# A decoder layer on one core: second norm in the drain of cross attention, a reordered first stage, and other banks for the side jobs of attention

## The reference

```
x = layernorm(x + ssm(x))              # xp = x W_in^T, dt = softplus(W_dt xp + b), a = exp(-dt exp(logA)), scan, W_out
x = layernorm(x + cross_attn(x, ctx))  # 16 heads, 8 kv heads, 1024 keys of width 256
h = x + self_attn(rmsnorm(x, w1))      # 16 heads, 4 kv heads, causal, rotary
x = layernorm(h + moe(rmsnorm(h, w2))) # 8 experts, 2 per row
```

## Time and profile before

| | us |
|---|---|
| three runs | 1571.29, 1569.46, 1571.0; median 1571.0 |
| profiled execution: its own time | 1574.32 |
| its span, first to last instruction | 1571.8 |
| mean granted TensorE clock | 0.942 |

### The profile page before, as it was taken

How to read it: one execution, slowest core, us unless ns; L and a number is a source line. 1 busy time by engine, 2 the same in 40 slices (tenths; PEclk the granted TensorE clock), 3 DMA queues, 4 the chain that set the end, 5 groups by cost and what they waited for, 6 DMA issues and landing times. The chain is left out here.

```text
span 1571.8 us, 25227 instructions
## 1 busy us (share of the span) xinstructions
PE 1387.9 (88%) x8067; PEld 740.1 (47%) x8067; DVE 1051.2 (67%) x1984; ACT 814.1 (52%) x1462; POOL 385.7 (25%) x585
## 2 busy tenths in 40 slices
PE   7888999999999999972879999997569999999971
PEld 4344444444444444431445555553336666666640
DVE  5747777777777777746577868785485655555654
ACT  5447666666666666633265656555244453444420
POOL 5302020201111110104464646542460000000024
PEclk9899999999999999985989999998779999999986
DMA  8217767575767676747234435344426454455334
GB/s 246 38 47 135 141 107 153 108 152 111 149 114 146 114 146 114 134 88 293 49 70 79 116 65 128 62 92 83 168 94 236 167 190 148 185 197 184 101 91 127
DMA packets 422079, 203.17 MB, mean 129 GB/s; under 512 B 369361, under 2 KB 383697, under 8 KB 422001
## 3 DMA queue, kind: packets, MB, share of 16 engines
q1 hardware_dynamic: 418224, 191.75, 50.4%
q0 software_dynamic: 3200, 10.49, 2.2%
q10 hardware_dynamic: 576, 0.00, 0.0%
HBM read 90.33 MB, written 18.55 MB: 69 GB/s over the span
## 5 line engine op out<-in xcount | busy, mean ns | idle before, releaser
L1188 DVE SCALAR_TENSOR_TENSOR xa_PN<-xa_SC,xa_rs,xa_PN 128x1024 f16<-128x1024 f32 x128 | 164.4, 1284 | 98.4 <-issue 97.7
L1076 ACT ACTIVATE xa_PN<-xa_SC,xa_rs 128x1024 f16<-128x1024 f32 x128 | 147.1, 1149 | 113.4 <-POOL xa_rs L916 113.4
L980 PE MATMUL xa_psS<-xa_KT,xa_QT 128*128 128x512 f16 x768 | 186.4, 379 | 6.4 <-DVE xa_mn L1201 5.0
L992 PE MATMUL xa_psO<-xa_PT,xa_V 128*128 128x512 f16 x768 | 173.5, 383 | 10.3 <-DMA xa_PT<-xa_PN 10.3
L916 POOL TENSOR_SCALAR xa_rs<-xa_rc,flag 128x1 f32<-128x1 f32 x128 | 34.2, 267 | 523.5 <-DVE xa_rc L1181 523.5
L1201 DVE CUSTOM_DVE_ANT_0 xa_SC<-xa_psS,maskb 128x1024 f32<-128x1024 f32 x128 | 155.2, 1212 | 4.5 <-PE xa_psS L980 2.4
L1098 ACT ACTIVATE xa_SC<-xa_SC,xa_mn 128x1024 f32<-128x1024 f32 x128 | 145.4, 1136 | 13.9 <-DVE xa_mn L1201 13.8
L1557 PE MATMUL rmoe_psG<-rmoe_XGT,W 128*128 128x352 f16 x768 | 126.8, 315 | 8.4 <-DVE rmoe_HF L1662 6.8
L1557 PE MATMUL rmoe_psU<-rmoe_XGT,W 128*128 128x352 f16 x768 | 125.6, 313 | 2.4 <-issue 2.4
L1572 PE MATMUL rmoe_psY<-W,rmoe_HT 128*128 128x512 f16 (+1 forms) x576 | 126.8, 379 | 0.0
L1662 DVE TENSOR_TENSOR rmoe_HF<-rmoe_psU,rmoe_SG 128x352 f32<-128x352 f32 x64 | 33.6, 525 | 137.5 <-ACT rmoe_SG L1614 133.3
(11 more groups left out here) (232 smaller groups left out, 2419.9 us busy)
## 6 DMA issues: line engine op xcount, KB each, us to landing
W13raw<-in_L_ffn_w_dram SPq DMA_DIRECT2D x16, 2048.0 KB, 12.1
W2raw<-in_L_ffn_w_dram SPq DMA_DIRECT2D x8, 2048.0 KB, 8.3
expert_rows_dram<-zeros SPq DMA_DIRECT2D x11, 512.0 KB, 8.7
xa_WPraw<-in_L_xattn_Wq_dram SPq DMA_DIRECT2D x8, 512.0 KB, 4.9
xa_WOraw<-in_L_xattn_Wo_dram SPq DMA_DIRECT2D x8, 512.0 KB, 4.5
sa_WPraw<-in_L_ffn_wq_dram SPq DMA_DIRECT2D x4, 1024.0 KB, 6.7
sa_WOraw<-in_L_ffn_wo_dram SPq DMA_DIRECT2D x4, 1024.0 KB
expert_out_dram<-rows SPq DMA_DIRECT2D x16, 256.0 KB, 2.2
```

The source lines that it names most:

```text
L980: last = nc.tensor.matmul(psS[j % NSC][:, c:c + cw], QT[b][:, hq, g, t * P:(t + 1) * P], KT[b][:, hk, c:c + cw], start=(q == 0), stop=(q = ...
L992: last = nc.tensor.matmul(psO[:, c:], V[b][:, hv, blk, :], PT[g % NPT][:, blk, hp, c:], start=(blk + q == 0), stop=(blk == NBLK - 1 and q ...
L1076: nc.scalar.activation(PN[j % NPN][:, 0:w // P, 0, :], by_block(SC[j % NSC], w), ACT.Identity, scale=rs[:, j % 4:j % 4 + 1]).then_inc(norm ...
L1188: nc.vector.scalar_tensor_tensor(out=PN[j % NPN][:, 0:w // P, 1, :], in0=by_block(SC[j % NSC], w), scalar=rs[:, j % 4:j % 4 + 1], in1=PN[j ...
```

## The change

Three things. (1) The first stage is reordered. DVE does the mask's work before the step that needs `WZ`; ACT casts all four pieces of `wout` early; POOL splits `xa_WP` before the context, and starts the last three of its four context pieces only when both `step_low` are done (a wait on `dt_lo`); eight buffers for `dec` (laid over `win` and `winN`) free batch 1's decays from batch 0's scans, and PE spreads batch 1's steps earlier. (2) The phase "n2" is gone. Its work is a tail of cross attention: batch 0's tiles are normed by DVE and POOL while the last `PN` tiles are turned; PE transposes them between `values` and the last output tiles; batch 1's tiles are normed as their output tiles are added. The square sum on ACT is replaced by arithmetic on the variance (one short POOL instruction more per tile, none on ACT). `sa_WP` is loaded in the last kv head's first half and split by ACT and POOL in the last half, steps 2 to 7. The copies of the normed tiles now precede the 14 DMAs of zeros in SP's list. `PN` and `CN` lie over `X2`, the copies' target. (3) The bank table of the side jobs differs between the batches, for both attentions, and in self attention three of the four `wo` jobs stand one step later.

```
-            for n in range(DC, 2 * DC):                                          # ACT
-                decay(n)
+                decay(DC + n)
...
+            for b in range(B):                                                   # POOL, after xa_WP
+                pool.wait_ge(c_in[b], 16)
+                for q in range(2):
+                    if b or q:
+                        pool.wait_ge(dt_lo, B)
...
-    BANK = (0, 1, 2, 0, 1, 2, 0, 1, 2, 1)
-    BACK = (3, 2, 3, 3, 3, 3, 3, 3, 3, 2)
+    BANK = ((0, 1, 2, 0, 1, 2, 0, 2, 1, 0), (2, 1, 0, 2, 1, 0, 2, 0, 1, 2))
...
-                 5: ([("proj", 4)], []), 6: ([("proj", 5)], []), 8: ([("wo", 0)], []), 10: ([("wo", 1)], []),
-                 12: ([("wo", 2)], []), 14: ([("wo", 3)], [])}
+                 5: ([("proj", 4)], []), 6: ([("proj", 5)], []), 9: ([("wo", 0)], []), 11: ([("wo", 1)], []),
+                 13: ([("wo", 2)], []), 14: ([("wo", 3)], [])}
...
+    def jobs_back(h, k, last):
+
+        if isinstance(h, int) and h == 1 and k < 2:
+            return k + 1
+        return 3 if last else (3, 3, 3, 3, 3, 3, 3, 2, 4, 3)[k]
...
+            if tail is not None:                                                 # SP
+                for t in range(TPB):
+                    sp.wait_ge(landed[t], 16 * 2 * kv_heads * groups)
+                for i in range(NT):
+                    sp.wait_ge(ln_done, i + 1)
+                    sp.dma_start(keep[:, i, :], X[:, i, :]).then_inc(kept, 16)
+                for dst, src, arrived in clear:
+                    sp.dma_start(dst, src).then_inc(arrived, 16)
+                sp.wait_ge(kept, 16 * NT)
...
+            if tail is not None:                                                 # PE
+                for i in range(TPB):
+                    norm_pe(pe, i)
             for t in range(TPB):
                 h = 2 * kv_heads - 1
-                output(h, 1, t, jobs_before(h) + JO + t, ring[(t + 1) % NJ])
+                output(h, 1, t, jobs_before(h) + JO + t, psJ[(1, 0, 2, 1)[t]])
+            if tail is not None:
+                for i in range(TPB, NT):
+                    norm_pe(pe, i)
...
             for t in range(TPB):                                                 # DVE
                 h = 2 * kv_heads - 1
-                output_add(h, 1, t, jobs_before(h) + JO + t, ring[(t + 1) % NJ])
+                output_add(h, 1, t, jobs_before(h) + JO + t, psJ[(1, 0, 2, 1)[t]])
+                if tail is not None:
+                    norm_stats(TPB + t)
+                    if 0 < t < TPB - 1:
+                        norm_apply(TPB + t - 1)
+            if tail is not None:
+                norm_dve(dve, TPB)
+                norm_apply(NT - 2)
+                norm_apply(NT - 1)
...
-            phase_norm(nc, "n2", X, identF, XT=XT, norm_w=norm1_w, keep=X2, fetch=loads + cleared)
...
+                          tail=(norm1_w, X2, own_weights, own_loads, cleared))
```

More of the change, by code:

```diff
@@ L427, in _ @@
                 tr_act(act, n)
-            for m in range(2, DC):
-                nc.scalar.copy(woutN[:, m, 0, :], wout[:, m, :]).then_inc(woutN_hi, 1)
             act.wait_ge(small_in, 32)
@@ L1125, in half @@
                         piece_high(*piece[:2])
+                    if last and tail is not None and 0 <= j - NWO < len(next_pieces):
+                        dst, src = next_pieces[j - NWO]
+                        if j == NWO:
+                            act.wait_ge(next_in, 16 * len(next_loads))
+                        nc.scalar.copy(dst[:, 0], src).then_inc(next_hi, 1)
             if not ready:
@@ L1142, in _ @@
                 pass
+            if tail is not None:
+                for i in range(NT):
+                    norm_act(act, i)
         @block.vector
@@ L1221, in half @@
                     jobs(h, b, j, first, last, 1)
+                    if last and tail is not None and j == NS:
+                        for i in range(TPB):
+                            norm_stats(i)
+                        for i in range(TPB):
+                            norm_apply(i)
             for i, (dst, src) in enumerate(wp_pieces if not ready else []):
@@ L1881, in decoder_layer @@
             cleared.append((YG[at:at + w, :], zeros[0:w, :], zeroed))
-        with ExitStack() as cross:
-            CT = cross.enter_context(nc.sbuf_tensor("CT", [P, 2, DCTX // P, B * S2], F16))
-            maskb = cross.enter_context(nc.sbuf_tensor("maskb", [P, B, S2], F32))
-            weights, loads = attention_weights(nc, cross, "xa", 2, DCTX // P, xWq, xWk, xWv)
-            phase_ssm(nc, X, XT, CT, x, ctxt, mask, W_in, W_out, log_A, W_dt, b_dt,
-                      (identF, causal, maskb, flag, ropeC, ropeS, zeros), rope_in, weights, loads)
-            attention(nc, "xa", X, XT, CT, identF, weights, xWq, xWk, xWv, xWo, 8, 2, S2,
-                      lambda b, t: maskb[:, b, :], flag, None, ready=True)
@@ L1891, in decoder_layer @@
[L1891 to L1898 removed]
+        X2 = sb("X2", [P, NT, D], F32)[:]
@@ new lines, in decoder_layer @@
+        with ExitStack() as own:
+            own_weights, own_loads = attention_weights(nc, own, "sa", 4, DC, wq, wk, wv)
+            with ExitStack() as cross:
+                CT = cross.enter_context(nc.sbuf_tensor("CT", [P, 2, DCTX // P, B * S2], F16))
+                maskb = cross.enter_context(nc.sbuf_tensor("maskb", [P, B, S2], F32))
+                weights, loads = attention_weights(nc, cross, "xa", 2, DCTX // P, xWq, xWk, xWv)
+                phase_ssm(nc, X, XT, CT, x, ctxt, mask, W_in, W_out, log_A, W_dt, b_dt,
+                          (identF, causal, maskb, flag, ropeC, ropeS, zeros), rope_in, weights, loads, X2)
+                attention(nc, "xa", X, XT, CT, identF, weights, xWq, xWk, xWv, xWo, 8, 2, S2,
+                          lambda b, t: maskb[:, b, :], flag, None, ready=True,
+                          tail=(norm1_w, X2, own_weights, own_loads, cleared))
+            attention(nc, "sa", X, XT, XT, identF, own_weights, wq, wk, wv, wo, 4, 4, S,
+                      lambda b, t: causal[:, S - (t + 1) * P:S], None, (ropeC, ropeS), ready=True)
```

163 lines of the change are left out of this document (115 added, 48 removed).

## The result

The changed kernel takes 1544.9 us (1544.7 to 1546.8, four runs) beside 1570.2 (1566.9 to 1571.3) on the same chip: a ratio of 0.984, 95% interval [0.9825, 0.9857], so 25.3 us less. The forecast was 1548, with a range of 1537 to 1558. The profiled execution took 1544.87, its span 1542.7 against 1571.8, the mean granted clock 0.951 against 0.942.

The account below looks back on a forecast made before the run. PE is about nine tenths busy, so only its waits or half-clock stretches count. First stage -7, boundary -15, weights' split +1, banks +1 and self attention -3 sum to -23: 1548 us against 1571.0, range 1537 to 1558.

Parts of the forecast that it names:

- First stage: Start of the kernel: earlier scans, decays and outputs from the reordering save 7 us, bounds -11 and -4.
- `scan_low`: First stage, before batch 1's scans: four DVE instructions beside POOL's context pieces take 7.5 us, between 3.3 and 8.
- mask work ahead of `WZ`: First stage: three DVE instructions moved to where DVE waited for `WZ` cost 0, or 1 if cover is short.
- Boundary: Cross attention's end to self attention's first projection: norm in the drain saves 15 us, bounds -25 and -11.5.
- the list: SP's 14 DMAs of zeros at the boundary, behind the last copy at 714.7: 13.3 us, SP through at 728.
- Weights' split and banks: Cross attention: splitting `sa_WP` beside the last half costs 1 us (0 to 3), the new banks 1 (0 to 4).
- Rival D: Cross attention: the job at k = 7 waits for a late V split; at 2 us a half +4, 1575; chance 0.05.
- Self attention: Later `wo` 0 fills part of each wait, -2, and a spared slow clock gives -1: -3, bounds +1 and -10.
- The clock's part: Self attention: a shorter wait may spare one group of slow matmuls after it, -1.
- rival C: Self attention keeps its clock in every half: another -7 there, 1541; chance 0.10.
- Rival A: SP's queue takes the zeros faster when empty, so the boundary gives -25: 1538; chance 0.14.
- Rival B: First stage gives nearly nothing, as POOL's context pieces run beside `scan_low` and outputs start late: -1, 1554; chance 0.15.

Follow-up runs that it names:

- a1: The changed kernel again, unaltered, on the chip where the first stage's single edits ran; 1545.5 us beside 1571.3 for the kernel before.
- m1: The changed kernel with the mask's instructions back in their old places in the first stage; 1547.4 us beside 1571.3 for the kernel before.
- h1: The changed kernel with the same bytes of zeros in 9 DMAs instead of 14; 1527.3 us beside 1558.9 for the kernel before.
- h2: The changed kernel with every second of the 14 DMAs of zeros issued by ACT, the others by SP; 1526.3 us beside 1558.9 for the kernel before.
- b1: The changed kernel with one bank table for both batches and the old distances, slots staying new; 1532.8 us beside 1558.9 for the kernel before.
- s1: The changed kernel with self attention's four `wo` jobs back at steps 8, 10, 12, 14; 1536.0 us beside 1557.2 for the kernel before.
- x1: The changed kernel without the mask's move, POOL's wait on `dt_lo`, and batch 1's early spread and decays; 1539.6 us beside 1558.9 for the kernel before.
- z1: The changed kernel with its 14 DMAs of zeros moved behind transposes in self attention's second half; 1520.8 us beside 1557.2 for the kernel before.
- o1: The changed kernel with two loops swapped, so SP issues the zeros before the eight copies; 1520.5 us beside 1557.2 for the kernel before.

## Why the prediction was right, and where it was off

The direction and its three sources hold, with the boundary as the largest; the time is 3.1 us below the forecast. By its own steps:

- **First stage, -7: -8.9.** By other pairs of profiles it is -6 to -11, as slow matmuls fall on one or the other. Scans at 39.1, as computed from the decays; batch 1's and the outputs within 1.5 us. The term that was mis-sized is `scan_low`, 7.5 us for four: they took 5.3. The price beside a neighbour was right or even low (1.44 and 2.60 us, where I had 1.9); the number was wrong. I had put a context instruction beside each of the four, but POOL did four of its six beside the decays and the scans, which they hardly slow (4.65 us for four scans; 4.55 for the next four, with POOL idle). By the Trainium skill (SBUF — State Buffer, section "SBUF: two separate sides") the port that DVE and GpSimd share is an exclusive lock, and I had worked out 9 us for four and -5 for the stage from it. The trace agrees with it as a mechanism: the first two `scan_low` end 0.54 us behind the context cast and the context subtraction that they met (45.09 against 44.55, 47.62 against 47.08). My sum by it failed by the same count. The mask work ahead of `WZ` was costed at 0 and delayed it by about 1 us (21.7 in a1, 20.9 in m1), inside its bound.
- **Boundary, -15: -11.7.** Compute was done 27.5 us behind `values` (27 to 27.8 forecast), the last copy was issued 23.7 behind it (23.5). The step that failed is the list: "five go at once (3.5 us) and nine at 1.1 to 1.28: 13.3 us". Four went in 3.6 us and ten at 1.3: 16.6, the 16.7 that the earlier trace rows had measured. I had made the queue emptier than before by what stood ahead of the zeros, and had taken the lowest rate of the range for the rest; but from the fourth DMA on an issue takes 1.3 us, with the gap behind it, as it did before. The row itself was the better forecast. The premise, that the queue takes the DMAs as the data moves, failed as well, in h1 and h2: 512 KB move in 1.37 us, and that an issue takes as long is a coincidence, since pieces of 1 MB are issued in 1.45.
- **Weights' split and banks, +1 and +1: +0.3 together**, and b1 gives the banks 0. Rival D's stall never came: the line of `xa_psJ<-xa_WO` had 0.0 us of idle time before it.
- **Self attention, -3: -8.3 in the profiles, about 4 by s1.** The waits fell by 2.3 (2 forecast). The clock's part was taken as -1 and is -6 between these two profiles; rival C had priced that. I had counted one group of slow matmuls as spared, where all four were, and the profile that I read showed more of them than the others do. One of the four is of projections, which no slot moved, and which runs slowly in x1 and h2 again: luck. That the shorter wait (1.9 instead of 2.2 us) is enough in every half is seen in eleven profiles; why it is, isn't shown, since in other places waits no longer than these were followed by slow matmuls.
- **Rival A, SP not held**, is refuted for the changed kernel, and z1 and o1 are what it would have looked like: 27.97 and 28.57 us from `values`, where it had 28.3. **Rival B** fell with the first stage. That the sum came within 3.1 us is in part luck: between the two profiles the boundary missed by +3.3 us and self attention by -5, and these cancel in part.

One sum stays open: taken from the timed runs, the norm in the drain is worth 25.5 - 6.2 - 4.3 = 15 us, from the traces 11.7. The difference is within the intervals of the three.

## What to carry to other kernels

Where a phase ends with a barrier, look at what the issuing queue still has to issue after its last dependent item; put what nobody waits for in front of the items for which the queue would stand waiting. Here swapping two loops gave 11 us on top of the 25 of the whole change. When a row measures exactly the DMAs in question, take its time, and argue it down only with a row that shows them faster.

## What was not expected of the hardware

- The bytes don't say how long a list of DMAs holds its engine: 14 DMAs with 6.5 MB hold SP for 16.6 us, 9 DMAs with the same bytes for 12.1, and two queues with 7 each for 7.9 (SP) and 8.6 us (ACT), all at 381 to 384 GB/s. Nor does a fixed number outstanding: at some 1.3 us an issue it was three in the changed kernel, and six in h1 and in the kernel before.
- A DVE instruction with two SBUF inputs that meets a POOL subtraction of 2.45 us takes 2.60 us in place of 0.68, at 32 partitions as at 128; a mean over four of them hides it. DVE's scans beside the same work lose 0.1 us in four.
- After equal waits of 2.21 us PE ran its next twelve matmuls in 2.76 or in 4.11 us, in one execution.
